# Side work of VectorE, GpSimd and ScalarE put into other units of the cross-attention loop of a two-layer decoder

## The reference, cut to what matters

```
# L1_attn: a long convolution along the sequence, per channel, then gelu, projection, affine layer norm
out = conv(x) + D_vec * x;  out = gelu(out) @ W_proj.T + b_proj
x3  = layer_norm(x + out) * gamma + beta;   x = _layernorm(x + x3)
# L1_xattn: 16 heads of width 16, every row attends to 77 context rows
q = x @ Wq.T + bq;  k, v from ctx_1024
attn = softmax(q k^T / sqrt(16));  out = (attn @ v) @ Wo.T + bo
x = _layernorm(x + out)
```

## Time and profile before

| | |
|---|---|
| three runs | 787.16, 781.5, 787.8 us, median 787.16 |
| profiled execution | 784.69 us, span 783.0 us |
| TensorE matmul busy | 713.0 us (91%) |
| VectorE busy | 505.3 us (65%) |
| ScalarE busy | 552.9 us (71%) |
| GpSimd busy | 194.4 us (25%) |
| chain that ended last, by engine | TensorE 56%, ScalarE 22%, VectorE 15% |

### The profile page before, as it was taken

The page is one execution under the profiler, slowest core; times in us unless marked ns, Lnnn a source line. Parts: engine busy times, 40 slices in busy tenths (PEclk is TensorE's granted clock), DMA queues, the critical chain, the costliest instruction groups (busy, mean ns, idle before and its releaser), DMA issues.

```text
span 783.0 us, 10853 instructions
## 1 busy us (share of the span) xinstructions
PE 713.0 (91%) x3850; PEld 387.3 (49%) x3850; DVE 505.3 (65%) x1181; ACT 552.9 (71%) x977; POOL 194.4 (25%) x246
## 2 busy tenths in 40 slices
PE   4999999989999999999999999889899999992797
PEld 2652222212222225888888886544455644440686
DVE  4794645753413224588647557979877687988776
ACT  3759999999999995464043345587687533898992
POOL 1661142201010000104253242465444100000022
PEclk9999999999999999999999999989899999996799
DMA  7412112141255160303326000010100000000002
GB/s 197 134 32 49 28 28 71 25 95 28 46 142 177 29 182 0 109 2 108 114 101 216 1 1 0 1 70 11 41 1 0 1 1 0 1 0 0 0 28 81
DMA packets 57389, 42.13 MB, mean 54 GB/s; under 512 B 36882, under 2 KB 54136, under 8 KB 57208
## 3 DMA queue, kind: packets, MB, share of 16 engines
q1 hardware_dynamic: 57192, 41.31, 19.1%
q10 hardware_dynamic: 144, 0.13, 0.1%
HBM read 28.59 MB, written 4.46 MB: 42 GB/s over the span
## 4 chain that ended last, share of the span: by engine, by line
PE 56%; ACT 22%; DVE 15%; issue 3%; DMA 1%; SPq 1%; POOL 1%; POOLq 0%; ACTq 0%; DVEq 0%
ACT arena L654 12%; PE banks L1658 8%; PE banks L2207 7%; PE banks L1962 7%; PE banks L1978 6%; PE banks L1644 4%; PE banks L1628 2%; PE banks L1992 2%; ACT arena L878 2%; DVE arena L1486 2%; DVE arena L1049 2%; ACT arena L879 2%; PE banks L1818 2%; ACT arena L867 1%; PE banks L2095 1%
## 5 line engine op out<-in xcount | busy, mean ns | idle before, releaser
L654 ACT ACTIVATE arena<-banks 128x1024 f32<-128x1024 f32 x256 | 239.7, 1047 | 6.5 <-PE banks L1658 4.1
L1658 PE MATMUL banks<-arena 128*32 128x512 f32 x1024 | 136.4, 604 | 2.6 <-DVE arena L1125 2.4
L1644 PE MATMUL banks<-arena 64*128 64x512 f16 x512 | 86.4, 383 | 10.1 <-ACT arena L654 5.8
L2207 PE MATMUL banks<-arena 128*128 128x512 f32 x192 | 83.1, 594 | 1.1 <-DVE arena L1502 0.9
L397 POOL TENSOR_SCALAR arena<-arena 128x2 f32<-128x2 f32 (+2 forms) x39 | 11.8, 302 | 256.2 <-DVE arena L1052 256.2
L1644 PEld LDWEIGHTS banks<-arena 64*128 64x128 f16 x512 | 20.9, 93 | 108.7 <-ACT arena L654 98.9
L777 ACT ACTIVATE arena<-banks,arena 128x77 f32<-128x77 f32 x256 | 59.3, 369 | 19.5 <-DVE arena L1402 19.5
L735 ACT ACTIVATE arena<-banks,arena 128x256 f32<-128x256 f32 x64 | 26.9, 471 | 49.3 <-PE banks L1962 49.3
L2207 PEld LDWEIGHTS banks<-arena 128*128 128x128 f32 x192 | 36.2, 190 | 47.4 <-issue 43.4
L1978 PE MATMUL banks<-arena 128*128 128x256 f32 x256 | 56.5, 380 | 1.2 <-ACT arena L676 1.2
L1962 PE MATMUL banks<-arena 128*128 128x256 f32 x256 | 56.2, 379 | 0.0
(11 more groups left out here) (263 smaller groups left out, 1258.4 us busy)
## 6 DMA issues: line engine op xcount, KB each, us to landing
arena<-in_L_ffn_w SPq DMA_DIRECT2D x16, 1024.0 KB, 7.4
w_kept<-arena SPq DMA_DIRECT2D x3, 768.0 KB, 3.6
arena<-w_kept SPq DMA_DIRECT2D x3, 768.0 KB, 4.7
arena<-in_x SPq DMA_DIRECT2D x4, 512.0 KB, 7.9
out_x<-arena SPq DMA_DIRECT2D x3, 512.0 KB, 2.9
arena<-in_L_ffn_b SPq DMA_DIRECT2D x1, 1024.0 KB, 9.2
arena<-in_L_ffn_w_gate SPq DMA_DIRECT2D x1, 768.0 KB, 7.8
arena<-in_L_ffn_w_up SPq DMA_DIRECT2D x1, 768.0 KB, 9.5
```

Of the source, the lines that this page charges most:

```text
L654: act.activation(PT[kt % 2][:, half], PS[:, 2 * (n % 3):2 * (n % 3) + 2, :], ACT.Exp, scale=DH ** -0.5 / QK_UP ** 2).then_inc(sem("exp_don ...
L1644: mm = pe.matmul(bank(2 * (n % 3) + h), KT[u % 2][64 * h:64 * h + 64, P * kt:P * kt + P], QT[u % 2][64 * h:64 * h + 64, 512 * half:512 * h ...
L1658: mm = pe.matmul(PS[32 * j:32 * j + 32, 6, :], VS[w][:, kt, h, :], PT[kt % 2][:, half, h, :], start=(kt == 0), stop=(kt == TB - 1))
L2207: mm = pe.matmul(bank(2 + n % 4), (wgT if n < IC * G4 else wuT)[:, k, P * c:P * c + P], XT[:, k, 512 * g:512 * g + 512], start=(k == 0), s ...
```

## The change

Only the place of work moves; every operation, its operands and their number stay. One call of `convolved` and both of `conv_affine` are cut in two between instructions.

- VectorE: the convolution of group 3 was in units 2 to 4 and is in 2 to 5; `x_stats(2)` goes from 7 to 6 and its `x_norm` from 9 to 7; `conv_out(3)` from 7 to 8; `conv_stats(3)` from 10 to 9; the two halves of `conv_affine(3)` from units 11 and 12 to 10 to 13, two tiles each; `x_stats(3)` from 13 to 15.
- GpSimd: `x_plus_bproj(3)` from unit 1 to 6, `x_plus_beta(3)` from 5 to 8, `x_plus_bo(1)`, `(2)`, `(3)` from 4, 12, 20 to 17, 20, 25. The `ln_power` steps of units 8, 11, 14 are in 6, 9, 15.
- ScalarE: both `conv_gelu(3)` from unit 5 to 7; `xT_evac(XA_N[2])` from after the exponentials of unit 10 to ahead of those of unit 11; the first group's `o_evac` from units 9, 10 to 10, 11.
- TensorE: `projected(3)` from unit 6 to 7; the first group's `xa_values` from 8, 9 to 9, 10; `x_turn4(2)` from 10 to 11.

```diff
+VALUES_AT = (1, 0, 0)
-XA_LN = {8: (LN_DN[5],), 11: (LN_DN[6],), 14: (LN_DN[7],), 17: (LN_E,), 23: (LN_E + 1,), 30: (LN_E + 2,)}
+XA_LN = {6: (LN_DN[5],), 9: (LN_DN[6],), 15: (LN_DN[7],), 17: (LN_E,), 23: (LN_E + 1,), 30: (LN_E + 2,)}
+XA_BO = (17, 20, 25)
...
-                if n == 1:
-                    x_plus_bproj(3)
-                if n == 5:
-                    x_plus_beta(3)
                 for step in XA_LN.get(n, ()):
                     ln_power(step, 4)
-                if n % 8 == 4 and n // 8 + 1 < G4:
-                    x_plus_bo(n // 8 + 1)
+                if n == 6:
+                    x_plus_bproj(3)
+                if n == 8:
+                    x_plus_beta(3)
+                if n in XA_BO:
+                    x_plus_bo(1 + XA_BO.index(n))
...
-                if m in (1, 2) and g >= 1:
-                    o_evac(g - 1, m - 1)
+                if g >= 1 and m - VALUES_AT[g - 1] in (1, 2):
+                    o_evac(g - 1, m - VALUES_AT[g - 1] - 1)
...
-                if n == 3:
-                    xT_evac(XA_N[1], 1, 6)
-                if n == 5:
+                if n in (3, 11):
+                    xT_evac(XA_N[g + 1], g + 1, 6)
+                if n == 7:
 
                     conv_gelu(3, 0)
                     conv_gelu(3, 1)
                 if n + AHEAD < UX:
                     numer(n + AHEAD)
-                if m == 2 and 1 <= g < G4 - 1:
+                if m == 2 and g == 2:
                     xT_evac(XA_N[g + 1], g + 1, 6)
...
-            between = {2: lambda: (convolved(3, 0, 0), convolved(3, 0, 1)), 3: lambda: convolved(3, 1, 0), 4: lambda: convolved(3, 1, 1),
-                       7: lambda: (conv_out(3), x_stats(2)), 9: lambda: x_norm(LN_DN[5], 2).then_inc(sem("ln_d2"), 1),
-                       10: lambda: conv_stats(3), 11: lambda: conv_affine(3, 0), 12: lambda: conv_affine(3, 1), 13: lambda: x_stats(3),
-                       14: lambda: residual(0, 0), 16: lambda: x_norm(LN_DN[7], 3).then_inc(sem("ln_d2"), 1),
-                       15: lambda: residual(0, 1), 17: lambda: xa_stats(0), 18: lambda: xa_norm(0),
+            between = {2: lambda: convolved(3, 0, 0),
+                       3: lambda: (convolved(3, 0, 1), convolved(3, 1, 0, (0,))),
+                       4: lambda: convolved(3, 1, 0, (1,)), 5: lambda: convolved(3, 1, 1),
+                       6: lambda: x_stats(2), 7: lambda: x_norm(LN_DN[5], 2).then_inc(sem("ln_d2"), 1),
+                       8: lambda: conv_out(3), 9: lambda: conv_stats(3),
+                       10: lambda: conv_affine(3, 0, (0, 1)), 11: lambda: conv_affine(3, 0, (2, 3)),
+                       12: lambda: conv_affine(3, 1, (0, 1)), 13: lambda: conv_affine(3, 1, (2, 3)),
+                       14: lambda: residual(0, 0), 15: lambda: (residual(0, 1), x_stats(3)),
+                       16: lambda: x_norm(LN_DN[7], 3).then_inc(sem("ln_d2"), 1),
+                       17: lambda: xa_stats(0), 18: lambda: xa_norm(0),
...
-                    if m < KD:
-                        xa_values(g - 1, m, range(NC5))
+                    if 0 <= m - VALUES_AT[g - 1] < KD:
+                        xa_values(g - 1, m - VALUES_AT[g - 1], range(NC5))
...
-                if m == (2 if g else 3) and g + 1 < G4:
+                if m == (2 if g == 2 else 3) and g + 1 < G4:
                     x_turn4(g + 1)
-                if n == 6:
+                if n == 7:
                     projected(3)
```

More of the change, by code:

```diff
@@ L1298, in kernels, with convolved @@
                 link(ins)
-            def convolved(g, k, part):
+            def convolved(g, k, part, steps=(0, 1)):
                 at = 4 * P * (g % 2)
@@ L1305, in convolved @@
                 if part == 0:
[L1306 to L1310, removed]
+                    if 0 in steps:
+                        dve.wait_ge(sem("xgT"), CONV_N[g] + 1)
+                        if g or k:
+                            dve.wait_ge(sem("conv"), KD * g + k)
+                        link(dve.tensor_tensor(conv_z, xt, Apow[:, k, at:at + 4 * P], ALU.mult))
+                    if 1 in steps:
+                        link(dve.tensor_tensor_scan(r, ones.to_broadcast([P, 4 * P]), conv_z, carry[:, k:k + 1] if g % 2 else 0.0, ALU.mult, ALU.add))
                 else:
@@ L1346, in conv_stats, with conv_affine @@
                 stats((lambda j: XB3[g][:, j, :], 4)).then_inc(sem("ln_stat"), 1)
-            def conv_affine(g, part):
+            def conv_affine(g, part, tiles=range(4)):
                 if part == 0:
@@ L1354, in conv_affine @@
                     dve.wait_ge(sem("x3_plus"), 2 * g + 2)
-                for j in range(4):
+                for j in tiles:
                     xb = XB3[g][:, j, :]
```

## The result

Over 20 runs each, the change has a median of 789.38 us (786.62 to 792.73) against 786.04 us (781.5 to 788.64): ratio 1.0045, 95% interval 1.0029 to 1.006. It is slower by 3.3 us. Of the runs behind the ratios, one of the kernel before (1772.94 us) and one of e3 (1410.24 us) stood far outside all others and are left out.

The account below looks back on a forecast made before the run. VectorE, slowed beside GpSimd, was taken to pace most units, with TensorE close. Lowest(22) at 573.4 against 571.70 and p_turn(21) at 577.8 against 576.70 gave +1.1 us; forecast 786.5 us, put between two bases, range 780 to 791.

Parts of the forecast that it names:

- Units 2 to 7, the convolution: VectorE's units 2 to 7: unit 6 starts 2 us earlier, but unit 7's norm waits 2.1 and 0.9 us for GpSimd.
- The gap and the projection: TensorE stands 4.9 us for unit 7's gelus, its clock falls, projection ends at 528.4 not 525.75; VectorE stands 3.5 us.
- Units 8 to 18: VectorE's own work 40.3 us plus 3.9 of waits for TensorE: lowest(22) at 573.4 against 571.70.
- The tail: After lowest(22): later units bound by TensorE; numer(22), q_evac(3) and evacuation bring p_turn(21) to 577.8 from 576.70, +1.1 us.
- From the sum to the number: Whole kernel: +1.1 us gives 785.8 on the profiled execution, 788.3 on the median; put between, 786.5.
- A: TensorE's clock holds through the gap before the projection, lowest(11) at 526.5: -1.6 us; chance 0.2.
- B: Units 2 to 18: clock holds and VectorE's halves and norms mostly miss GpSimd's instructions: about -6.5 us; chance 0.15.
- C: TensorE's clock stays at 1.2 GHz for a second piece after the projection: 3.4 us more, +4.5; chance 0.15.
- D: Whole kernel: a shift in the units is absorbed and nothing moves, 0 us; chance 0.08.

Follow-up runs that it names:

- e3: The change with both gelus in ScalarE's unit 6 and x_plus_bo(1) and (2) on GpSimd in units 19 and 21; ratio 0.998 to the kernel before.
- e4: The change with 11 added matmuls filling TensorE's gap ahead of projected(3), results unchanged; ratio 1.0 to the kernel before.
- e8: The change with both conv_affine(3) whole again, in VectorE's units 11 and 12; ratio 1.0037 to the kernel before.
- e2: The change with GpSimd's x_plus_bo(1) and (2) in units 19 and 21 in place of 17 and 20; ratio 0.9978 to the kernel before.
- e1: The change with both gelus in ScalarE's unit 6 in place of 7; ratio 1.0012 to the kernel before.
- e5: The change with 11 added matmuls in TensorE's gap and x_plus_bo(1) and (2) in units 19 and 21; ratio 0.9966 to the kernel before.
- e6: The change with gelus in unit 6, conv_out(3) ahead of group 2's norm, GpSimd's additions in 5, 6, 19, 21, 25; ratio 0.9941 to the kernel before.
- e9: The change with GpSimd's additions back in units 1, 5 and 4, 12, 20; ratio 1.003 to the kernel before.
- e11: The kernel before with only GpSimd's additions moved, to units 5, 6, 19, 21, 25; ratio 0.9911 to the kernel before.
- e7: The kernel before with only GpSimd's additions moved, to the change's units 6, 8, 17, 20, 25; ratio 1.0019 to the kernel before.
- e10: The kernel of e7 run once more, unchanged; ratio 0.9989 to the kernel before.

## Why the prediction was right or wrong

- **Units 2 to 7, the convolution.** Right. Units 2 to 6 summed to 19.1 us in my working and take 19.3 (505.73 to 525.02); the norm of unit 7 was to take 2.1 + 0.9 + 1.38 = 4.4, and took 4.22.
- **The gap and the projection.** Right in cause and size. Gap 4.9 forecast, 5.09 measured; VectorE's stand 3.5 and 3.65; the table load 1.28 and 1.28; the fall 2.7, by e4 2.5.
- **Units 8 to 18.** Right. `lowest(22)` at 573.4 - 500.63 = 72.8, measured 72.76. VectorE's own work was put at 40.3 us and its waits at 3.9; they are 40.8 and 3.2. The cut of the affine, which I charged with two more waits of 0.9, cost nothing that e8 could show: where VectorE was done sooner, it stood longer.
- **The tail.** This step failed. "Later units are bound by TensorE, so what arrives there counts" carried +1.1 to `p_turn(21)`, where +1.3 arrived, and stopped. I had worked out that `numer(22)` no longer lay under `queries(3)`, which is a stand of TensorE, and did not ask of it what I had asked of the first gap. It was 2.69 us, the clock fell for 3.4 us, and of the 2.9 us at the end (285.25 less 282.33) 1.6 were lost behind `p_turn(21)`. e2 takes the stand away and 3.6 us with it: 2.0 of the norm and the 1.6. The stand of 2.69 or 2.70 us was followed by a fall in all four profiles that have it (the change, e1, e4, e8); in e2, e3, e5, e6 and e9, where it is 0.68 or 0.69, no fall is there. So the sum should have been near +2.9.
- **From the sum to the number.** This step failed too, and it turned the sign. My sum was +1.1 us, but the number, 786.5, lay 0.7 below the median shown, since I put it between two bases, and so a sum of one sign became a number of the other. 20 runs put the base at 786.04; with +1.1 on it the forecast would have been 787.1, with +2.9 788.9. I also took 1% for about what a measurement can tell from no change; 20 runs told 0.45%.
- **Rivals.** A and B are out, the clock fell. C put the loss at a longer fall behind the projection; it fell for one piece there, and the second piece came 58 us later, behind another stand. Its +4.5 is nearer to the measured +3.3 than my +1.1, but not for its reason. D is out, the interval does not hold 1.
- **The causes, weighed.** Two things carry the loss: the gelus directly ahead of the projection, by the fall in the gap (ratio 1.0 once it is filled, e4), and `x_plus_bo(1)` behind the inverse root (0.9978 once it is moved, e2). Both together give 0.9966 (e5). The addition behind the other inverse root, `x_plus_bproj(3)`, lengthened its norm to 4.22 as well but cost nothing in the change, since VectorE then stood for the projection anyway: with the norm at 2.23 in e9 that stand was 5.57 in place of 3.65. What the change gained, the free L1313 and the affine without an addition beside it, is real but was spent. Not tried alone: the gelus and the projection moved on the kernel before.

## What to carry to other kernels

List, for each long instruction of one engine, which operations of the other it meets, and move it to where it meets none: e11 moved five additions of about 2.4 us and gained 0.9%. e6, which has GpSimd's additions in the same units and all the moving of VectorE's and ScalarE's work besides, gained 0.6%; whatever this work is worth beside the additions, the runs do not show it. When a consumer and the work that it waits for stand in the same unit, count the stand of the consumer in full. Then price every stand of TensorE that the change makes or lengthens twice, with the clock held and with it fallen, at each such place down to the end, and let a profile of more than one execution say how often it falls. Keep the number on the base that the sum was made for.

## What the runs showed of the hardware

- The clock is not a property of the kernel alone. One kernel (e7, e10) ran its cross-attention with no fall and with two; the distance to the end was 280.09 and 285.88 us. Single profiles of such kernels cannot rank changes of 2 us at the end; the runs can. The mean granted clock of a run shows the same: on the chips of the experiments 23 runs of the kernel before with a mean of 0.976 took 783.3 to 785.8 us, and 8 with 0.970 took 789.2 to 789.8.
- The stand of 5.09 us on TensorE had the granted clock at 0.5 from its last part on (the change, e2, e8); one of 1.27 us did not (e1, e3, e6); 2.46 us did in one execution of two. In e9 the clock fell at 514.3, at a stand of only 1.74 us, ahead of the long one. Filled with 11 matmuls, the gap kept 1.00 in both profiles that have them (e4, e5).
- The length of a stand alone does not tell a fall. One of 3.50 us near 18 to 22 us was followed by a piece in the change and not in e3, and the second piece of the kernel before began in one of 1.46 us. In e3 and e11 a piece of 3.4 us began right behind two stands of 1.1 and 0.45 us (597.2 and 589.7) that the other eleven profiles have too, and pass at 1.00.

```profile
21.88 3.78 PE L1638 MATMUL banks<-arena 128*128 128x512 f32 x4 [3.50 <-ACT arena L605]
```

The same place in e3:

```profile
21.68 1.98 PE L1638 MATMUL banks<-arena 128*128 128x512 f32 x4 [3.50 <-ACT arena L605]
```

And the kernel before, where its second piece begins at 554.7:

```profile
555.20 1.40 PE L2048 MATMUL banks<-arena 64*128 64x308 f32 x4 [1.46 <-ACT arena L777]
```

- A norm of four instructions took 1.38 us alone, 2.23 to 2.27 beside a `weights` and 4.22 to 4.30 beside an addition and a `weights`; 3.1 where it came late to the addition (e1, e3). Among the operations that wait, the wait is set by what GpSimd runs: beside a `weights` it is 0.85 us for the norm (2.23 less 1.38) and 0.87 for the scan (2.12 less 1.25), and the reduces L1407 do not wait at all (0.76 to 0.80).
